# Second cross-attention of a small decoder: gate and low-rank products at other turns, and an end of the stage in an order of its own

## What is computed

```python
# cross-attention, 8 heads of 128
q = (x @ Wq) * SCALE;  k = (context @ Wk) * SCALE;  v = context @ Wv      # per head
attn = softmax(einsum('bqhc,bkhc->bhqk', q, k))
x = layernorm(x + einsum('bhqk,bkhc->bqhc', attn, v) @ Wo + bo)
# feed-forward: a base product, and a low-rank one weighed by gates (8 experts, rank 8)
result = x @ base_w.T + base_b
gating = softmax(x @ router_w.T + router_b).astype(bfloat16)
mid    = x @ lora_A
x = layernorm(x + result + einsum('bsr,erd,bse->bsd', mid, lora_B, gating) * 2)
```

## Time and profile before

| | us |
|---|---|
| median of 3 runs (lowest, highest) | 1099.26 (1098.34, 1099.91) |
| the profiled execution | 1098.13 |
| its span, first to last instruction | 1096.3 |
| PE busy | 998.7 |
| PE weight loads busy | 773.7 |
| DVE busy | 586.3 |
| ACT busy | 410.3 |
| POOL busy | 150.6 |

### The profile page before, as it was taken

The page is one execution under the profiler, slowest core; times in us unless marked ns, Lnnn a source line. Parts: engine busy times, 40 slices in busy tenths (PEclk is TensorE's granted clock), DMA queues, the critical chain, the costliest instruction groups (busy, mean ns, idle before and its releaser), DMA issues. The chain is left out here.

```text
span 1096.3 us, 17961 instructions
## 1 busy us (share of the span) xinstructions
PE 998.7 (91%) x6656; PEld 773.7 (71%) x6656; DVE 586.3 (53%) x1319; ACT 410.3 (37%) x1065; POOL 150.6 (14%) x151
## 2 busy tenths in 40 slices
PE   6899699999999999869999996688789999999985
PEld 4578577777777777569999994355576776676563
DVE  2786545555555556656655554477325444544543
ACT  2556433333333334335444522366423222322221
POOL 0334311011011000014343422100100000000000
PEclk9999899999999999979999997899799999999997
DMA  4500000000000000074121000600100000001000
GB/s 146 186 2 1 29 15 1 16 15 1 14 0 0 0 0 0 1 242 117 46 70 38 0 1 1 135 1 2 46 1 15 15 15 15 14 2 27 4 6 13
DMA packets 24286, 34.34 MB, mean 31 GB/s; under 512 B 3168, under 2 KB 19888, under 8 KB 24224
## 3 DMA queue, kind: packets, MB, share of 16 engines
q1 hardware_dynamic: 24224, 33.51, 10.3%
HBM read 30.75 MB, written 2.75 MB: 31 GB/s over the span
## 5 line engine op out<-in xcount | busy, mean ns | idle before, releaser
L1028 ACT ACTIVATE x_prob<-bank,x_negmax 112x375 f32<-112x375 f32 x128 | 72.3, 570 | 153.2 <-DVE x_negmax L944 153.2
L1778 DVE TENSOR_TENSOR moe_h_low<-moe_sq,moe_h_high 128x448 fp32r<-128x448 f32 x64 | 54.8, 873 | 52.8 <-ACT moe_h_high L1843 39.6
L1819 POOL TENSOR_TENSOR moe_sq<-moe_r 128x448 f32<-128x448 f32 x64 | 64.2, 1005 | 122.3 <-ACT moe_r L1851 103.8
L86 PE MATMUL bank<-moe_w_low,moe_h_high 128*112 128x256 f32 x256 | 71.8, 281 | 0.0
L86 PE MATMUL bank<-moe_w_high,moe_h_high 128*112 128x256 f32 x256 | 71.7, 280 | 0.0
L86 PE MATMUL bank<-moe_w_high,moe_h_low 128*112 128x256 f32 x256 | 71.7, 280 | 0.0
L944 DVE TENSOR_REDUCE x_negmax<-bank 112x1 f32<-112x375 f32 x128 | 64.1, 543 | 7.7 <-PE bank L836 5.7
L1851 ACT ACTIVATE moe_r<-bank 128x448 f32<-128x448 f32 x64 | 35.0, 546 | 86.6 <-PE bank L86 84.9
L1521 ACT ACTIVATE x_prob<-bank,x_negmax 112x375 f32<-112x375 f32 x64 | 36.1, 569 | 76.4 <-DVE x_negmax L1382 76.4
L949 DVE COPY x_prob_t<-bank 125x336 f32<-125x336 f32 x128 | 59.0, 499 | 5.7 <-PE bank L845 3.8
L857 PEld LDWEIGHTS bank<-x_prob_t,x_v 125*64 125x64 f32 x768 | 37.2, 136 | 33.9 <-issue 29.9
(11 more groups left out here) (360 smaller groups left out, 2281.0 us busy)
## 6 DMA issues: line engine op xcount, KB each, us to landing
moe_w<-in_L_ffn_W SPq DMA_DIRECT2D x16, 512.0 KB, 4.7
ctx_t<-in_ctx_t SPq DMA_DIRECT2D x8, 376.0 KB, 4.7
x_ctx_t<-in_ctx_t SPq DMA_DIRECT2D x8, 376.0 KB, 3.4
wk<-in_L_xattn_Wk SPq DMA_DIRECT2D x2, 1024.0 KB, 6.7
wv<-in_L_xattn_Wv SPq DMA_DIRECT2D x2, 1024.0 KB, 9.4
wq<-in_L_xattn_Wq SPq DMA_DIRECT2D x2, 1024.0 KB, 11.5
wo<-in_L_xattn_Wo SPq DMA_DIRECT2D x2, 1024.0 KB, 13.3
w_in<-in_L_attn_W_in SPq DMA_DIRECT2D x1, 1160.0 KB, 6.9
```

The source lines that it names most:

```text
L86: last = pe.matmul(out, lhs, rhs, start=(k == 0), stop=(k == len(pairs) - 1))
L1028: act.activation(PROB(u, e)[:, :], S_BANK(u, e)[0:T, 0:S], ACT.Exp, bias=negmax[:, g:g + 1], accum_out=total[:, g:g + 1]).then_inc(p_ready, 1)
L1778: dve.tensor_tensor(h_low[half][:, m, :], sq[m % 2][:, :], h_high[half][:, m, :].bitcast(F32), ALU.subtract).then_inc(low_done, 1)
L1819: pool.tensor_tensor(sq[m % 2][:, :], r[m % 2][:, :], r[m % 2][:, :], ALU.mult).then_inc(sq_done, 1)
```

## The change

In the rounds:

- GATES of item i - 3 moves from turn 1 to turn 2, ahead of the first half's weighting, where LOW stood;
- LOW moves from turn 2 of round i + 3 to turn 0 of round i + 4, ahead of the second half's weighting of the item before;
- `gates` on VectorE moves from turn 0 to turn 1, `add_low` to turn 0 of the next round, `finish` from turn 3 to turn 1 of the next round; on ScalarE `gate_exps` goes ahead of turn 0's exponentials, `end_deviation` to turn 1, and in turn 2 the copy of NT goes ahead of the exponentials.

All three loops end with round 7. What is left then is written out as an order of its own: TensorE does NT of item 6, the last weighting, OUT 7, LOW 4, BASE 6, GATES 5, NT 7, BASE 7, LOW 5, GATES 6, GATES 7, LOW 6, LOW 7.

The core of the diff:

```diff
     def jobs(i, u, at):
-        if i > B:
-            return {(1, MID): [(GATES, B - 2), (GATES, B - 1)], (2, MID): [(LOW, B - 2), (LOW, B - 1)]}.get((u, at), [])
...
-        if u == 1 and at == MID and i > 2:
+        if u == 2 and at == MID and i > 2:
             return [(GATES, i - 3)]
-        if u == 2 and at == MID and i > 2:
-            return [(LOW, i - 3)]
+        if u == 0 and at == MID and i > 3:
+            return [(LOW, i - 4)]
         if u == 3 and at == LATE and i > 1:
-            return [(BASE, i - 2)] + ([(NT, i - 1), (BASE, i - 1)] if i == B else [])
+            return [(BASE, i - 2)]
         return []
 
+    first_left = [(NT, B - 2)]
+    left = [(OUT, B - 1), (LOW, B - 4), (BASE, B - 2), (GATES, B - 3), (NT, B - 1), (BASE, B - 1), (LOW, B - 3), (GATES, B - 2),
+            (GATES, B - 1), (LOW, B - 2), (LOW, B - 1)]
...
+                for job_ in first_left:
+                    job(job_)
+                weigh(B - 1, 1)
+                for job_ in left:
+                    job(job_)
...
             @block.vector
-                for i in range(B + 1):
+                for i in range(B):
                     for u in range(J):
...
+                        if u == 0 and i > 3:
+                            add_low(i - 4)
                         if u == 0 and i > 0:
                             collect(i - 1, 1)
                         if u == 3 and i > 0:
                             normalize(i - 1)
-                        if u == 2 and i > 2:
-                            add_low(i - 3)
                         if after:
                             normalize_heads(*after)
-                        if u == 0 and i > 2:
+                        if u == 1 and i > 2:
                             gates(i - 3)
-                        if u == 3 and i > 2:
-                            finish(i - 3)
+                        if u == 1 and i > 3:
+                            finish(i - 4)
...
+                collect(B - 1, 1)
+                gates(B - 3)
+                residual(B - 1)
+                add_low(B - 4)
+                base(B - 2)
+                normalize(B - 1)
+                finish(B - 4)
                 gates(B - 2)
                 base(B - 1)
+                add_low(B - 3)
                 gates(B - 1)
-                for i in (B - 2, B - 1):
-                    add_low(i)
-                for i in (B - 2, B - 1):
-                    finish(i)
+                finish(B - 3)
+                add_low(B - 2)
+                add_low(B - 1)
+                finish(B - 2)
+                finish(B - 1)
...
             @block.scalar
+                        if u == 2:
+                            drain_all(jobs(i, u, EARLY))
+                        if u == 0 and i > 2:
+                            gate_exps(i - 3)
                         if after:
                             exps(*after)
-                        if u == 0 and i > 2:
-                            gate_exps(i - 3)
+                        if u != 2:
+                            drain_all(jobs(i, u, EARLY))
+                        drain_all(jobs(i, u, MID))
...
+                        if u == 1 and i > 3:
+                            end_deviation(i - 4)
...
+                drain_all(first_left)
+                gate_exps(B - 3)
+                collect(B - 1, 1)
+                deviation(B - 1)
+                end_deviation(B - 4)
                 gate_exps(B - 2)
+                drain((GATES, B - 3))
+                drain((NT, B - 1))
                 gate_exps(B - 1)
-                for i in (B - 2, B - 1):
-                    drain((GATES, i))
-                for i in (B - 2, B - 1):
-                    end_deviation(i)
+                end_deviation(B - 3)
+                drain((GATES, B - 2))
+                drain((GATES, B - 1))
+                end_deviation(B - 2)
+                end_deviation(B - 1)
```

More of the change, by code:

```diff
@@ L1076, in jobs @@
     def jobs(i, u, at):
-        if i > B:
-            return {(1, MID): [(GATES, B - 2), (GATES, B - 1)], (2, MID): [(LOW, B - 2), (LOW, B - 1)]}.get((u, at), [])
         if u in (0, 1, 3) and at == EARLY:
             m, a = i // 2 + 1, i % 2 * 3 + (0, 1, None, 2)[u]
-            return [(QUERY, m, a)] if m < B // 2 and i < B else []
+            return [(QUERY, m, a)] if m < B // 2 else []
         if u == 0 and at == LATE and i + 1 < B:
@@ L1317, in _ @@
                     prepare(len(first) + n, job_)
-                for i in range(B + 2):
+                for i in range(B):
                     for u in range(J):
-                        if i < B and u + 1 < J:
+                        if u + 1 < J:
                             scores(i, u + 1)
-                        elif i + 1 < B and u + 1 == J:
+                        elif i + 1 < B:
                             scores(i + 1, 0)
@@ L1325, in _ @@
                             job(job_)
-                        if i < B:
-                            turn(i, u)
+                        turn(i, u)
                         for job_ in jobs(i, u, MID):
                             job(job_)
-                        if u == 0 and 0 < i <= B:
+                        if u == 0 and i > 0:
                             weigh(i - 1, 1)
-                        if u == 2 and i < B:
+                        if u == 2:
                             weigh(i, 0)
@@ L1564, in _, with drain_all @@
                 on_vector = (OUT, BASE, LOW)
-                for i in range(B + 1):
+                def drain_all(jobs_):
+                    for job_ in jobs_:
+                        if job_[0] not in on_vector:
+                            drain(job_)
+                for i in range(B):
                     for u in range(J):
                         after = following(i, u)
+                        if u == 2:
+                            drain_all(jobs(i, u, EARLY))
+                        if u == 0 and i > 2:
+                            gate_exps(i - 3)
                         if after:
                             exps(*after)
-                        if u == 0 and i > 2:
-                            gate_exps(i - 3)
-                        for job_ in jobs(i, u, EARLY) + jobs(i, u, MID):
-                            if job_[0] not in on_vector:
-                                drain(job_)
+                        if u != 2:
+                            drain_all(jobs(i, u, EARLY))
+                        drain_all(jobs(i, u, MID))
                         if u == 0 and i > 0:
                             collect(i - 1, 1)
-                        if u == 2 and i > 2:
-                            end_deviation(i - 3)
-                        if u == 2 and i < B:
+                        if u == 1 and i > 3:
+                            end_deviation(i - 4)
+                        if u == 2:
                             collect(i, 0)
@@ L1582, in _ @@
                             deviation(i - 1)
[L1583 to L1585 removed]
+                        drain_all(jobs(i, u, LATE))
+                drain_all(first_left)
[3 more added lines that the diff above has]
+                end_deviation(B - 4)
                 gate_exps(B - 2)
+                drain((GATES, B - 3))
+                drain((NT, B - 1))
                 gate_exps(B - 1)
[L1588 to L1591 removed]
+                end_deviation(B - 3)
[3 more added lines that the diff above has]
+                end_deviation(B - 1)
 def norm_statistics(dve, chain, core, mv, stats, pad, ready):
```

12 lines of the change are left out of this document (4 added, 8 removed).

## The result

The changed kernel takes 1090.54 us (1089.46 to 1092.16), the one before 1099.74 us in the same comparison: a ratio of 0.9914, 95% interval 0.9895 to 0.9934, or 7 to 12 us. A second comparison on another chip gave 0.9910 (0.9882 to 0.9939). One of the six launches of the kernel before took 2431.24 us: it stands outside the ratio, and moves that kernel's median by 0.2 us. The time lies inside the range, 1.4 us under the 1091.9 that were predicted.

A forecast was written before the change was run, and what follows sets the result against it. TensorE, busy 998.7 of 1096.3 us, was taken to bound the kernel, so only its waits and the end could gain. Rounds 6.95 + 1.06 + 0.61 = 8.62, less 1.2: 1099.26 - 7.4 = 1091.9 us, range 1089.3 to 1094.8.

The forecast's parts named there:

- The wait of LOW: Turn 2, rounds 3 to 7: TensorE's wait for ScalarE's copy of xt goes, 1.39 x 5 = 6.95 us gained.
- for restarting the pipeline: Round 3 against round 2: 0.25 us of LOW's 1.39 that no row calls idle.
- The margin: Turn 2: NT's copy frees the shared bank in time for GATES, with 0.1 to 0.2 us to spare.
- GATES out of turn 1: Rounds 3 to 7: CTX_MAIN's wait goes (1.02), round 6 gains 0.56, 0.52 paid; together 1.06 us gained.
- The floor: Rounds 6 and 7: scores to scores need time for row maximum and both exponentials, 4.23 us by round 7.
- LOW at turn 0: LOW one round later, behind QUERY: its wait costs 0; four LOWs in the rounds, not five, gain 0.61 us.
- The end: After the rounds: 1.9 us later behind the last BASE, less 0.7 earlier at NT 7; 1.2 us lost.
- The clock: In the end: same fall to 1.2 GHz assumed; staying up gains 2.6 us, falling before BASE 6 loses 1.5.
- C: Rival: waits return at LOW behind QUERY or at GATES, at most 6.1 us given back, 1093.4 to 1098; chance 0.15.
- D: Rival: round 7's floor rules all rounds, so nothing is won, 1098 us; chance 0.04.
- E: Rival: VectorE has no room in turns 0 and 1 for 10.3 us of moved pieces, slower, 1102.2; chance 0.04.
- B: Rival: the clock stays at its high level in the end, 1089.3 us; chance 0.09.

The follow-up runs named there:

- e1_copy_late: Changed kernel, but ScalarE takes the copy of NT and every other EARLY job behind the two exponentials again: 1100.51 us, ratio 1.0009 to the kernel before.
- e2_copy_alone: Kernel before with one edit: in turn 2 ScalarE takes the copy of NT ahead of the exponentials; 1094.32 us, ratio 0.9941 to the kernel before.
- e3_gates_turn1: Changed kernel with GATES back at turn 1 and VectorE's gates back at turn 0: 1094.57 us, ratio 0.9958 to the kernel before.
- e5_again: Changed kernel once more, unedited, on another chip: 1091.35 us, ratio 0.9910 to the kernel before.
- e8_own_bank: Changed kernel with NT 6 behind the last weighting, LOW 5 ahead of the last BASE, OUT 7 in its own bank behind LOW 4: 1087.92 us, ratio 0.9878.
- e9_bank_filled: e8_own_bank with 11 unread products in TensorE's pauses from BASE of item 5 on: 1087.84 us, ratio 0.9875 to the kernel before.

## Why the prediction was right, point by point

The direction and the size come out by its own steps, with two terms a little off that offset each other.

- **The wait of LOW** (6.95): the mechanism is confirmed, the size was too high. No wait for xt is left in the rounds, e1_copy_late brings 6.78 back, but the wait alone, in e2_copy_alone, was worth 6.07: 1.21 a round, not 1.39. The 0.25 "for restarting the pipeline", found as what was left over between rounds 2 and 3, was 0.07 for LOW (1.21 less the 1.14 that its row shows) and 0.22 for GATES (6.78 / 5 = 1.36, less the same 1.14, in e1_copy_late). That the rounds came out right all the same is in part luck: GATES takes 0.16 from start to start at its new place, where the sum left it at 0.26 to 0.28, and LOW took 0.1 more than its 0.61 away with it from turn 2 (0.75 behind the transposes, GATES 0.65).
- **The margin** of GATES, 0.1 to 0.2: it held. In rounds 3 to 7 of every trace with GATES in turn 2 and the copy in its new place, GATES starts 0.10 to 0.12 behind the end of that copy, and the copy starts 0.03 to 0.05 behind the shown end of NT. So the modelled ends of matmuls were good enough for it, and what the Trainium skill says of them (Perfetto Trace Analysis, Tensor Engine Instruction) changed nothing here.
- **GATES out of turn 1** (1.06): confirmed by e3_gates_turn1, 1.26; it is more since GATES is cheaper in turn 2, as said. The floor, read from one row of round 7, was met to 0.01 us in round 6.
- **LOW at turn 0** (0.61 gained, no wait): nearly. The rounds gained 8.30, not 8.62. The 0.3 are missing in rounds 6 and 7, where LOW starts 0.84 behind the transposes of turn 0 (1005.52 and 1006.36), 0.1 later than the 0.74 that the weighting or BASE needs behind them, and the weighting takes 0.1 longer behind it than behind the transposes. In rounds 4 and 5 LOW takes 0.76 at turn 0, not 0.61, and what makes up for it was not in the sum: a gap of 0.13 ahead of QUERY in that turn is gone.
- **The end** (1.2 lost): 0.78 measured. In the old clock less 7.26, I had the weighting at 1060.59, OUT at 1065.09 and the residual at 1070.5; they came at 1060.57, 1065.04 and 1070.49. NT of item 7 came 0.25 sooner than summed, and the clock fell one step later (NT 0.41, not 0.63), 0.2. Behind BASE it was 6.72 against 6.7.
- **The clock** was the term that I had in part wrong. I asked whether it would fall around the last BASE, and it did so, as assumed. I had not asked it of the 2.57 us pause that the new order puts ahead of the last weighting, although the sum itself had found that pause. From the start of NT to OUT of item 7 it is 4.72 us in the changed kernel's first trace. With the fall it is 6.16 and 6.29 in e5_again and e3_gates_turn1, 1.4 and 1.6 more, where the clock was back within the weighting's first part, and 7.65 in e1_copy_late, 2.9 more, where it was back only within the second. It is inside the range, but belongs in the sum with a chance of its own. That the first trace of the changed kernel was one without it is luck: 7.4 us were predicted and 7.5 measured over the stretch, but with e5_again's it would be 6.1.
- **Rivals.** C (waits come back elsewhere), D (the floor rules all rounds) and E (VectorE has no room) are excluded by the table of rounds: VectorE's later pieces left no trace in it. B's state, a clock that stays up, was made by filling: worth 2.60 us, as priced.

The medians moved by 9.2 us, the stretch by 7.5. The interval of the ratio (7.3 to 11.5 us) holds both, and what makes the difference is not shown. Since the start of the stretch lies anywhere between 863.9 and 868.4 us in twelve traces of the same code, a difference of 1.7 us between two medians can come from there. Whether the ends of the kernel before lose to the clock more often than the one profiled is left open.

## What to carry to other kernels

Where several kinds of work share one bank, read who empties it and what stands ahead of that copy on its engine: moving a 0.35 us copy ahead of two 0.57 us exponentials brought three quarters of what the rounds gained, and can be had by one edit. Once a wait is gone, the next limit can often be read from a round that already shows it, as round 7 did. A cost found by subtracting one round from another takes in all that differs between them; a run that takes the one thing away sizes it. In an end like this one, count the pauses of TensorE as places where the clock may fall, and look for work, or a second bank, that closes them.

## What the hardware showed beyond that

The granted clock of the same program fell in a 2.57 us pause in one trace (e5_again) and not in another (after). Where it fell, it did so 1.8 (e1_copy_late), 2.1 (e5_again) and 2.4 us (e3_gates_turn1) after TensorE had stopped. The time of this end differs by it between executions: the first part of the last weighting took 2.45, 3.70, 3.84 or 4.71 us. In e2_copy_alone it fell within OUT of item 7, behind pauses of at most 1.18 us, and OUT took 7.12 instead of 5.43; the same pauses stand in the trace of the kernel before, where it did not fall there. With a few unread products in the pauses (six in a row took 1.47 us) the clock stayed up to the last LOW in the one trace of each of the three kernels that had them (that LOW took 0.68, 0.68 and 0.80). Where e8_own_bank and e9_bank_filled can be compared, at steps that both ran at the high clock, the filling delayed nothing by more than 0.01 us: from the last BASE to GATES of item 6 it is 1.76 and 1.77.
